# Decoder layer, mixing stage: path sums in two halves, the causal mask later, one path's sum on POOL, square roots on ACT

## The reference

```python
delta_path = delta_rule(q, k, v, beta)           # chunks of 32 tokens
paths = stack([fir3(v), fir15(v), fir64(v), delta_path, v])
stats = [mean, mean of squares, mean of |.|, sqrt(sum of squares)] of each path, head and token
logits = gelu(concat(x, stats) @ gW1 + gb1) @ gW2 + gb2
probs = softmax(logits / tau) * keep + eps
o = einsum('blhp,blhpd->blhd', probs, paths)
o = o * rsqrt(mean(o * o) + 1e-5) * norm_w
x = layernorm(x + o @ Wo)
```

## Time and profile before

| | us |
|---|---|
| median of 3 runs | 2091.64 |
| fastest and slowest of them | 2087.59, 2106.17 |
| the profiled execution's own time | 2096.82 |
| its span in the trace | 2095.1 |
| mean granted clock of PE in it | 0.794 of full speed |

### The profile page before, as it was taken

One profiled execution on the slowest core, in us unless ns is written; L12 is line 12 of the kernel. 1 busy time (PEld: TensorE's weight loads), 2 busy tenths in 40 slices (PEclk: granted clock), 3 DMA queues, 4 the chain that ended last, 5 costly groups with the idle time before them and its releaser, 6 DMA issues. The chain is left out here.

```text
span 2095.1 us, 27839 instructions
## 1 busy us (share of the span) xinstructions
PE 1568.9 (75%) x8700; PEld 1231.9 (59%) x8701; DVE 1011.6 (48%) x1987; ACT 634.0 (30%) x1261; POOL 647.8 (31%) x481
## 2 busy tenths in 40 slices
PE   5786838957888888830788888888826899999861
PEld 2554537956666766620677777877413566666630
DVE  4565639915766666640565555555401122122155
ACT  3231306954444444420222222222200122222212
POOL 4645550004555455540211221122271000000066
PEclk9676755558888787865898888988867999999975
DMA  4425335434222222109310111000221012112134
GB/s 112 136 82 160 100 92 152 131 117 96 71 66 59 57 70 70 41 10 334 110 37 24 29 35 35 25 27 28 74 105 48 28 55 59 56 55 60 52 111 146
DMA packets 188436, 165.21 MB, mean 79 GB/s; under 512 B 70400, under 2 KB 160096, under 8 KB 187488
## 3 DMA queue, kind: packets, MB, share of 16 engines
q1 hardware_dynamic: 129024, 100.29, 17.7%
q10 hardware_dynamic: 53216, 47.49, 6.9%
q0 software_dynamic: 6144, 16.79, 2.6%
HBM read 98.45 MB, written 56.62 MB: 74 GB/s over the span
## 5 line engine op out<-in xcount | busy, mean ns | idle before, releaser
L2125 POOL DMA_INDIRECT gathered<-outs,row_of_token x64 | 62.4, 975 | 423.4 <-POOLq L139 404.9
L1383 PE MATMUL attend_psum<-ctxT_tile,w_src 128*128 128x128 f32 x512 | 91.4, 353 | 62.0 <-ACT x_tile L1483 62.0
L2067 DVE TENSOR_TENSOR hidden<-unit_psum,gate 128x352 f32<-128x352 f32 x72 | 37.8, 525 | 206.7 <-ACT gate L2042 206.7
L654 PE MATMUL fir_psum<-window,toep 96*96 96x128 f32 x512 | 116.7, 401 | 23.3 <-DMA toep<-in_fir 21.1
L654 PEld LDWEIGHTS fir_psum<-window,toep 96*96 96x96 f32 x512 | 111.7, 257 | 28.2 <-DMA window<-value 20.5
L667 ACT ACTIVATE filtered<-fir_psum 32x512 f32 (+1 forms) x192 | 112.9, 588 | 46.9 <-PE fir_psum L654 42.2
L1383 PEld LDWEIGHTS attend_psum<-ctxT_tile,w_src 128*128 128x128 f32 x512 | 87.2, 265 | 64.5 <-issue 63.2
L2022 PE MATMUL unit_psum<-wd,hiddenT 128*128 (+1 forms) x432 | 111.9, 395 | 10.6 <-issue 9.8
L346 PE MATMUL proj_psum<-xT_block,wqkv 128*128 128x512 f32 x192 | 97.7, 662 | 26.0 <-DMA xT_block<-in_xT 22.5
L1216 POOL TENSOR_TENSOR path_stats<-path_stats,plus_half 128x40 f32<-128x40 f32 x16 | 108.7, 6796 | 25.4 <-DVE path_stats L1097 25.4
L479 DVE SCALAR_TENSOR_TENSOR conv_acc<-proj_psum,conv_taps,conv_acc 128x508 f32<-128x508 f32 (+1 forms) x144 | 96.2, 735 | 38.3 <-ACT conv_acc L401 38.3
(11 more groups left out here) (267 smaller groups left out, 3692.0 us busy)
## 6 DMA issues: line engine op xcount, KB each, us to landing
gate_part<-in_gw1s SPq DMA_DIRECT2D x8, 1280.0 KB, 10.7
rows<-zero_row ACTq DMA_DIRECT2D x9, 1024.0 KB, 10.4
unit_rows<-rows SPq DMA_DIRECT2D x72, 128.0 KB, 2.3
outs<-unit_out ACTq DMA_DIRECT2D x72, 128.0 KB, 2.5
ndg<-decay_gram ACTq DMA_DIRECT2D x8, 1024.0 KB, 7.1
neg_decay_gram<-ndg SPq DMA_DIRECT2D x16, 512.0 KB, 4.5
ctxT_tile<-in_ctxT SPq DMA_DIRECT2D x32, 256.0 KB, 3.5
window<-value SPq DMA_DIRECT2D x32, 192.0 KB
```

The lines of the kernel that those rows point to most:

```text
L654: mm = pe.matmul(psum[0:NFIR * QUART, u, TC * w + c, :], toep[:, w, :, :, c].rearrange("p f t -> p (f t)"), window[:, u, :, :, TC * w + c] ...
L1383: pe.matmul(psum[:, u, FRONT, m * L:m * L + L], w_src[:, k, m * 128:m * 128 + 128], cT[:, u, k, :], start=(k == 0), stop=(k == NK - 1))
L2125: pool.indirect_dma_start(out=got[:, b % NBUF, i, :], out_offset=None, in_=M.outs_dram[:, :], in_offset=bass.IndirectOffsetOnAxis(ap=M.pla ...
```

## The change

1. DVE's `path_sums` is cut into `path_sums(0)` (tile 0 of the pair) ahead of `sum_paths`, and `path_sums(1)` behind `mix_norm`.
2. `mask_scores` goes from ahead of `sum_paths` to behind `path_sums(1)`, still ahead of `scale_mix`.
3. POOL's `weight` writes the weighted value to a tile of its own (`own`), takes it ahead of the filtered paths, and then adds it to the weighted delta path in one operation on 128x512, after a wait on its own products. `weighted` is signalled by that add. DVE's `sum_paths` loses its last add (L1148).
4. `norms` moves from POOL's power to a Sqrt on ACT, between `keep_rows(1)` and `keep_rows(2)`.

```diff
@@ scalar
+            def norms(j, u):
+                i = 2 * j + u
+                act.wait_ge(ssq_made, i + 1)
+                act.activation(stat[:, u, :, :, 3], stat[:, u, :, :, 1], ACT.Sqrt).then_inc(norms_made, 1)
...
             staged_pair_loop(act, PAIRS, (square_delta, 2), (keep_cross, 1), (keep_rows(0), 1), (keep_rows(1), 1),
-                             (keep_rows(2), 1), (square_mix, 3), (keep_rows(3), 1), (square_paths, 1), (copy_stats, 2),
+                             (norms, 2), (keep_rows(2), 1), (square_mix, 3), (keep_rows(3), 1), (square_paths, 1), (copy_stats, 2),
@@ vector
-            def path_sums(j, u):
-                i = 2 * j + u
-                if not is_early(j, u, 2):
-
-                    dve.wait_ge(statsT_mm, i - 1)
-                for t in range(P):
+            def path_sums(t):
+
+                def step(j, u):
+                    i = 2 * j + u
+                    if t == 0 and not is_early(j, u, 2):
+
+                        dve.wait_ge(statsT_mm, i - 1)
                     fir, val = filtered_heads(M, tile(j, u, t)), value_heads(M, tile(j, u, t))
                     for s, mag in ((0, False), (2, True)):
                         dve.tensor_reduce(stat[:, u, t, 0:12, s], fir, AX.XY, ALU.add, apply_absolute_value=mag)
                         dve.tensor_reduce(stat[:, u, t, 16:20, s], val, AX.XY, ALU.add, apply_absolute_value=mag)
+                return step
...
                 ins.then_inc(mix_step, 1)
-                dve.wait_ge(mix_step, 2 * i + 1)
-                dve.tensor_tensor(mixed[:, :, :], mixed[:, :, :], delta[:, u, :, :], ALU.add).then_inc(mix_step, 1)
-                dve.wait_ge(mix_step, 2 * i + 2)
-                own = mixed[:, :, :].rearrange("p b (k c) -> p b k c", c=FC)
-                dve.tensor_tensor(own, own, M.value[:, :, pairs(j, u), :].rearrange("p k b c -> p b k c"),
-                                  ALU.add).then_inc(mix_summed, 1)
+                dve.wait_ge(mix_step, i + 1)
+                dve.tensor_tensor(mixed[:, :, :], mixed[:, :, :], delta[:, u, :, :], ALU.add).then_inc(mix_summed, 1)
...
-            staged_pair_loop(dve, PAIRS, (delta_sums, 2), (square_sums, 2), (mask_scores, 1), (sum_paths, 3), (mix_norm, 3),
-                             (path_sums, 1), (scale_mix, 3), (scale_delta, 1), (residual, 3), (shift_logits, 2), (ln_shift, 3),
-                             (probabilities, 2))
+            staged_pair_loop(dve, PAIRS, (delta_sums, 2), (square_sums, 2), (path_sums(0), 1), (sum_paths, 3), (mix_norm, 3),
+                             (path_sums(1), 1), (mask_scores, 1), (scale_mix, 3), (scale_delta, 1), (residual, 3), (shift_logits, 2),
+                             (ln_shift, 3), (probabilities, 2))
@@ gpsimd
-            def norms(j, u):
-                i = 2 * j + u
-                pool.wait_ge(ssq_made, i + 1)
-                pool.tensor_tensor(stat[:, u, :, :, 3], stat[:, u, :, :, 1],
-                                   wide(M.plus_half[:, 0:1].broadcast_to([128, NP * H]), [128, P, NP * H], 1),
-                                   ALU.pow).then_inc(norms_made, 1)
...
-                    own = delta[:, u, t, :].rearrange("p (h k c) -> p h k c", k=HK, c=FC)
-                    for paths, f0, nf in ((own, 3, 1), (filtered_heads(M, n), 0, 3), (value_heads(M, n), 4, 1)):
-                        ins = pool.tensor_tensor(paths, paths, prob(f0, nf), ALU.mult)
-                ins.then_inc(weighted, 1)
+                    def split(ap):
+                        return ap.rearrange("p (h k c) -> p h k c", k=HK, c=FC)
+
+                    for out, paths, f0, nf in ((split(delta[:, u, t, :]), split(delta[:, u, t, :]), 3, 1),
+                                               (split(own[:, t, :]), value_heads(M, n), 4, 1),
+                                               (filtered_heads(M, n), filtered_heads(M, n), 0, 3)):
+                        ins = pool.tensor_tensor(out, paths, prob(f0, nf), ALU.mult)
+                ins.then_inc(own_weighted, 1)
+                pool.wait_ge(own_weighted, i + 1)
+                pool.tensor_tensor(delta[:, u, :, :], delta[:, u, :, :], own[:, :, :], ALU.add).then_inc(weighted, 1)
...
-            staged_pair_loop(pool, PAIRS, (weight, 3), (norms, 2), (make_rhs, 0), (mix_inverse, 3), (ln_inverse, 3))
+            staged_pair_loop(pool, PAIRS, (weight, 3), (make_rhs, 0), (mix_inverse, 3), (ln_inverse, 3))
```

More of the change, by code:

```diff
@@ L732, in mix_paths @@
         mix_r = sb("mixed_inverse_norms", [128, P * H])
+        own = sb("own_weighted_value", [128, P, D])
         mixed = sb("mixed", [128, P, D])
@@ L774, in mix_paths @@
         probs_done = signal("probs_done")
+        own_weighted = signal("own_paths_weighted")
         weighted = signal("paths_weighted")
```

## The result

| | before | after |
|---|---|---|
| median of 4 runs each, us | 2094.43 | 2146.6 |
| fastest and slowest, us | 2087.59, 2106.17 | 2131.94, 2149.64 |
| profiled execution, us | 2096.82 | 2146.88 |
| mean granted clock of PE | 0.794 | 0.784 |

The change makes the kernel 2.3% slower: ratio 1.0229, 95% interval 1.0162 to 1.0296. The prediction was 2103, with a range up to 2124. The direction was right, the size wrong by a factor of four or five (+52 us measured, +11.6 worked out).

A forecast was written before the change was run, and what follows sets the result against it. A mixing-stage turn was taken as DVE's chain up to mixedT plus PE's clock-dependent tail. 14 full turns x 0.9 us - 1.0 for the last turns = +11.6 us, giving a median of 2103 us, range 2083 to 2124.

The forecast's parts named there:

- Norms on ACT: Square root between two keep_rows: its table load hides in ACT's wait for PE; cost 0, up to 1.6 us without cover.
- POOL's own sum: POOL's new 128x512 add takes 1042 ns, bounds 0.6 and 2.1 us; DVE waits 0.17 us for it.
- DVE's order: DVE's chain with halved path_sums, shorter sum and later mask: scale_mix ends at 796.76, a full 1 us earlier.
- One stop in place of two: PE ahead of delta_rows: one stop of 5.85 us replaces 1.75 + 2.86 = 4.61, +1.24 us per turn.
- PE's tail: delta_rows through logits: clock back 5.7 us after PE resumes, tail ends at 807.1 against 806.43; +0.9 us per turn taken.
- The bound that I had worked out: Upper bound for PE's tail: clock not back before logits, hidden_stats and output at 3.4 us each, +2.7 us per turn.
- My own remark: PE resumes with thin work, delta_rows and transposes; given as reason to take +0.9 us per turn, between +0.7 and +1.1.
- The last turns: Last two turns, without delta_rows: shorter chain to mix_inverse in turn 17, +0.35 us in turn 18; -1.0 us in all.
- Rival B: Mixing stage: the longer PE stop makes the slow clock the rule; +24 us if half the turns, +37 if all; chance 0.20.
- A: Favoured case, a small loss in the mixing stage: +0.4 to +1.4 us per turn, 2092 to 2111 us; chance 0.62.
- The signs that I named: Wrong if delta_rows skips the mask wait, mixedT-on tail is over 2 us off 8.6, or clock shifts beyond few hundredths.

The follow-up runs named there:

- norms_alone: Kernel before with only the norms moved from POOL to a square root on ACT: 2042.3 us against 2034.1, ratio 1.003.
- wide_first: Changed kernel with 8 unread 128x256 matmuls behind the wait for the mask, ahead of delta_rows: 2088.9 us against 2033.1 for before, single run.
- thin_first: Kernel before with 16 unread 128x64 matmuls behind the wait for scale_mix, ahead of mixedT: 2146.0 us against 2033.1 for before, single run.
- mask_mid_filled: mask_mid with unread 128x256 matmuls on PE, 6 ahead of delta_rows and 4 ahead of mixedT: 1975.6 us against 2033.1 for before, ratio 0.972.
- mask_back: Changed kernel with only the mask put back, ahead of the first half of path_sums: 2026.3 us, ratio 0.996 to before.
- mask_late_alone: Kernel before with only the mask moved behind path_sums, directly ahead of scale_mix: 2090.4 us against 2034.1, ratio 1.032.
- before_filled: Kernel before with unread 128x256 matmuls in PE's two stops, 5 ahead of delta_rows and 11 ahead of mixedT: ratio 0.993 to before.
- mask_mid: Changed kernel with the mask between sum_paths and mix_norm: 2077.6 us against 2091.2 for before, ratio 0.992.
- after_half_filled: Changed kernel with 9 unread 128x256 matmuls on PE in the stop ahead of delta_rows: 2099.5 us against 2091.2 for before, single run.
- mask_back_filled: mask_back with unread 128x256 matmuls on PE, 2 ahead of delta_rows and 11 ahead of mixedT: ratio 1.005 to before.

## Why the prediction was wrong, point by point

- **Norms on ACT cost 0**: right. The load starts at 785.23 inside ACT's wait, the Sqrt follows at 786.52 with no drain between, and `keep_rows(2)` starts at 786.83, 0.1 to 0.2 us behind PE. norms_alone has the turn of before. The drain of the Trainium skill ("ScalarE: Activation LUTs", on what a table load costs) is not in this trace.
- **POOL's own sum**: I took 1042 ns, it takes 1.27 us. DVE waits 0.37 us, under the 0.5 named.
- **DVE's order**: right. From the start of `square_sums` (782.75 here, 782.88 before) the removed add, the halves and the mask came out within 0.15 us of the working: `scale_mix` began 13.2 us later, as worked out.
- **One stop in place of two**: right in kind, `delta_rows` waits for the mask and `mixedT` for nothing. The term was +1.24 us per turn and measured +1.60, from 4.64 to 6.24. The turn that I read has one stop of 6.39 us, where I had worked out 5.85, in place of the two that add up to 4.61.
- **PE's tail**: this is the step that failed. I let `delta_rows` take 2.80 us and the clock come back "as long after that as here, 5.7 us". In the shown turn `delta_rows` took 3.65 us, the clock came back after 11.1, and from `mixedT` to the end of `logits` it was 9.3 us (800.05 to 809.38) where I had worked out 7.6 (799.5 to 807.1). So the gain that was to pay for part of the longer stop wasn't there: instead of 0.34 us less work time per turn (0.9 - 1.24) there was 1.29 more. The bound that I had worked out, +2.7 per turn for a clock that is not back before `logits`, was close to the true case in every turn, not the edge. My own remark that `delta_rows` and the transposes are thin work for PE to resume on named what wide_first and thin_first then showed; I had given it 0.2 us. The 2.80 of the earlier trace rows was a mixture of both levels and should not have been used as the low one; it was taken from a turn in which the clock fell behind the start of `delta_rows`, and the longer stop moves that start behind the fall.
- **The last turns**: -1.0 booked. From the last full turn's `mixedT` to the last of all it was 50.9 us before and 50.2 after.
- **Rival B** had the right mechanism, the slow clock through the tail in all turns, and at +37 the right price (the stage lost 40), with a chance of 0.20. It blamed the length of the stop alone, though, and wide_first has the same stop with a return after 3.3 us.
- **The range of A** doesn't follow from its terms: +0.4 to +1.4 per turn gives 2096 to 2110, not 2092 to 2111. The signs that I named would not have caught the miss either: from `mixedT` on it is 9.4 us, within 2 us of 8.6, and the mean clock over the full turns went from 0.80 to 0.77. The growth lies ahead of `mixedT`, in the stop and in `delta_rows`.
- **Slower by 7 us more in the cross-attention**: not in the prediction. From the first to the last start of its score products it takes 439 us in the kernel before, 446 to 447 in the kernel after, in norms_alone and in mask_mid_filled, and 435 to 436 in mask_back, mask_late_alone and before_filled, which hold quite different parts of the change. It is the clock again: over that stretch the mean granted clock is 0.89 before and 0.87 after, PE is busy for 379.7 and 388.3 us, and its idle time is 59.7 and 58.1; norms_alone has 0.87 too, mask_back 0.89. Why the clock is lower there isn't shown. It goes with no edit that I tried, so the 2.3% holds some 0.3% that may be chance of this pair of programs.

Left open is what exactly makes PE's clock fall and return: it fell around stops of 2.3 us in most turns but not in all, it fell in before_filled without a stop, and in mask_late_alone it returned after 7 or after 12 us in turns that look alike.

## What to carry to other kernels

When a step is moved on one engine, look at what the other engine's in-order queue has behind the wait, and then at what that engine resumes with; here, behind a stop of the same length, the clock was back after 3.3 to 4.8 us with 256-column products first and after 10.7 to 11.7 with 64-column ones. Price a tail at both levels of the clock, and if nothing in the trace settles which it will be, put the slow one in the middle of the range and not at its edge. Where an engine waits for another anyway, as DVE did for ACT's squares, a step put there costs less: a turn is 26.5 us with the mask there and 27.2 with the mask ahead of the path sums.

## What the runs showed of the hardware that I had not expected

- With a stop of 6.4 us, PE's granted clock came back 3.3 us after it resumed with matmuls of 128x256, and 11.1 us after it resumed with matmuls of 128x64 and transposes (wide_first and the kernel after). It was still at its lower level behind 6.9 us of 128x64 products (thin_first). With a stop of 8.2 us and the 128x64 products first it came back after 6.6 to 12.7 us (mask_late_alone).
- The granted clock also fell, for some 3 us in each of eight turns, while PE was never idle for longer than 0.1 us (before_filled).
- Work that nobody needs made the kernel faster: 10 matmuls per turn, 4.6 us of PE time, took 3.3 us off each turn of mask_mid.
- The Trainium skill ("TensorE: Matmul & The Clock Gate", on oscillation) warns of stops over about 3 us. Here the clock fell 0.1 to 2.1 us after PE's restart from a single stop of 2.0 to 2.5 us in 20 of the 22 turns that had one (9 of 11 in after_half_filled, 11 of 11 in mask_back_filled).
- POOL's add of two 128x512 tiles takes 1.27 us, its product of two such tiles 1.04.
